# Rows handed one by one into the preparation of the second and fourth graph layers, folded score vectors, and one block for the first layer's preparation

## What is computed

```python
for L in range(4):
    x = x + gnn[L](layernorm(x), adj, ...)
    x = x + ffn[L](layernorm(x), ...)      # top 2 of 16, 8, 8, 16 experts
```

```python
# layer 1, 4 heads of 64
h = x @ W.T; e = leaky_relu((h . a_src)[:, None] + (h . a_dst)[None, :], 0.2)
out = softmax(where(adj > 0, e, -inf)) @ h
# layer 3, twice: with e and with -e
h = x @ W;  e = leaky_relu(h @ a[:256] + (h @ a[256:]).T, 0.2)
out = elu(concat(softmax(e) @ x, -softmax(-e) @ x) @ wtrans)
```

## Time and profile before

| | |
|---|---|
| median of 3 runs | 1176.76 us (1168.61 to 1181.09) |
| the profiled execution, its own time | 1179.99 us |
| its span, first to last instruction | 1178.3 us |
| busy PE, DVE, ACT, POOL over the span | 953.0, 717.9, 491.4, 450.4 us |
| granted TensorE clock, mean | 0.894 of full |

### The profile page before, as it was taken

How to read it: one execution, slowest core, us unless ns; L and a number is a source line. 1 busy time by engine, 2 the same in 40 slices (tenths; PEclk the granted TensorE clock), 3 DMA queues, 4 the chain that set the end, 5 groups by cost and what they waited for, 6 DMA issues and landing times. The chain is left out here.

```text
span 1178.3 us, 23190 instructions
## 1 busy us (share of the span) xinstructions
PE 953.0 (81%) x7338; PEld 885.7 (75%) x7338; DVE 717.9 (61%) x1674; ACT 491.4 (42%) x926; POOL 450.4 (38%) x464
## 2 busy tenths in 40 slices
PE   5785978628788959884998999999658994999993
PEld 1584878625688959873898989999645883899992
DVE  4686555484777655656664546665454786466664
ACT  2151655400555526651204467776414451244341
POOL 1152664310877626640032015553103542344541
PEclk9795998959888669997998999999869996999997
DMA  6005865320000042746224001129420004656853
GB/s 233 1 28 175 294 217 175 115 63 1 6 10 10 6 162 73 254 139 202 62 86 166 11 14 36 45 64 341 166 77 1 10 14 179 250 171 199 283 182 125
DMA packets 63164, 136.85 MB, mean 116 GB/s; under 512 B 10704, under 2 KB 41200, under 8 KB 58352
## 3 DMA queue, kind: packets, MB, share of 16 engines
q1 hardware_dynamic: 54064, 111.24, 27.6%
q0 software_dynamic: 9024, 24.65, 6.9%
HBM read 201.64 MB, written 17.56 MB: 186 GB/s over the span
## 5 line engine op out<-in xcount | busy, mean ns | idle before, releaser
L1694 PE MATMUL r_pH<-e_xsT,e_w 128*128 128x128 f32 x2304 | 283.2, 281 | 25.0 <-DMA e_w<-w_in 16.3
L1694 PEld LDWEIGHTS r_pH<-e_xsT,e_w 128*128 128x128 f32 x2304 | 273.1, 197 | 28.7 <-issue 28.4
L1648 POOL DMA_INDIRECT y_rows<-e_ys,e_to x94 | 150.7, 1603 | 229.2 <-DVE e_idx L1791 109.3
L1803 DVE TENSOR_TENSOR e_w_lo<-e_w,e_w_hi 128x1024 fp32r<-128x1024 f32 (+1 forms) x94 | 137.8, 1466 | 41.5 <-ACT e_w_hi L1751 31.7
L451 PE MATMUL g_o<-g_V,g_pT 128*128 128x65 f32 (+2 forms) x896 | 145.6, 320 | 4.1 <-ACT g_pT L410 4.1
L1709 PE MATMUL r_pY<-e_w_hi,e_h_hi 128*128 128x256 f32 x464 | 140.9, 304 | 7.1 <-issue 6.3
L1658 POOL DMA_INDIRECT e_xs<-xn_rows,e_idx x94 | 105.3, 1120 | 99.5 <-DVE e_idx L1791 73.6
L1751 ACT ACTIVATE e_w_hi<-e_w 128x1024 fp32r<-128x1024 f32 (+1 forms) x94 | 117.1, 1246 | 62.1 <-DMA e_w<-w_in 60.8
L451 PEld LDWEIGHTS g_o<-g_V,g_pT 128*128 128x128 f32 x896 | 132.8, 208 | 11.8 <-ACT g_pT L410 5.1
L1709 PE MATMUL r_pY<-e_w_lo,e_h_hi 128*128 128x256 f32 x464 | 132.7, 286 | 0.0
L1709 PE MATMUL r_pY<-e_w_hi,e_h_lo 128*128 128x256 f32 x464 | 132.4, 285 | 0.0
(11 more groups left out here) (303 smaller groups left out, 1668.1 us busy)
## 6 DMA issues: line engine op xcount, KB each, us to landing
e_w<-w_in SPq DMA_DIRECT2D x56, 1024.0 KB
e_w<-w_in SPq DMA_DIRECT2D x84, 512.0 KB
e_w<-w_in SPq DMA_DIRECT2D x52, 514.0 KB
e_w<-w_in SPq DMA_DIRECT2D x24, 1028.0 KB
e_b<-b_in SPq DMA_DIRECT2D x76, 128.0 KB
e_w<-y_rows SPq DMA_DIRECT2D x32, 256.0 KB, 5.3
p_adj<-adj_in SPq DMA_DIRECT2D x8, 512.0 KB, 7.2
xn_rows<-xn SPq DMA_DIRECT2D x32, 128.0 KB, 1.7
```

The lines of the kernel that those rows point to most:

```text
L1648: pool.indirect_dma_start(out=y_rows[:, :], in_=ys[b][:, :], in_offset=None, out_offset=bass.IndirectOffsetOnAxis(ap=to[b][:, :], axis=0))\
L1694: ins = nc.tensor.matmul(pH[b % 2][:, f, :], w1[b][:, at:at + P], xsT[b % 2][:, c, :], start=(c == 0), stop=(c == DC - 1))
L1803: nc.vector.tensor_tensor(w2_lo[b % 2][:, :], w2[b][:, :], w2_hi[b % 2][:, :].bitcast(F32), ALU.subtract).then_inc(w2_split, 1)
```

## The change

1. Layer 0: constants and preparation are one block. SP issues x, Wn1, neighT, Wv, Wx1, Wfx and the adjacency; ACT issues the 19 small loads on its own queue. PE starts with a run of 64 matmuls on ones, takes neighT's network first, and puts the value matmuls between the transposes. Values and the passed-on half of x are taken from one PSUM tile by instructions over all 8 row tiles.
2. Layer 0's experts to layer 1 (`BeforeGraph1`) and layer 2's experts to layer 3 (`BeforeGraph3`): the weights of the next graph layer are loaded before the wait for the last stores. The weighted sum, the norm, the transposes and the projections then run row tile by row tile at the end of the expert block. The preparation blocks are gone.
3. Layer 1's score vectors are folded into the weights: 4 small matmuls make `wa`, and the dst rows come from xnT by 8 matmuls of 128 columns for each tile (`wab`). hT is no longer computed. ACT empties PSUM in place of DVE. POOL does the power, one column at a time; DVE adds eps.
4. Layer 3: V is projected in the handover, not at the head of the attention block.
5. w1_own, w2_own and b2_own (layer 2) share one tile, in which layer 3's V later lies.

Layers 1 to 2 and the end keep their sum as it was (`PlainSums`, `LastLayer`).

```diff
+class WeightedSum:
...
+def add(self, dve, link, t, acc, base):
+    dve.wait_ge(self.loaded[t], 16)
+    link(nc.vector.scalar_tensor_tensor(out=acc, in0=self.yg[t][:, 0, :], scalar=wts[:, 0, t:t + 1],
+                                        in1=base, op0=ALU.mult, op1=ALU.add))
+    nc.vector.scalar_tensor_tensor(out=acc, in0=self.yg[t][:, 1, :], scalar=wts[:, 1, t:t + 1],
+                                   in1=acc, op0=ALU.mult, op1=ALU.add).then_inc(self.ready, 1)
...
+class Handover:
...
+    def rows(self, dve, link):
+        for t in range(NT + 1):
+            if t < NT:
+                self.sums.add(dve, link, t, x[:, t, :], x[:, t, :])
+                dve.wait_ge(self.sums.ready, t + 1)
+                self.norm.moments(dve, t)
+            if t >= 1:
+                self.norm.norm(dve, t - 1)
+    def gpsimd(self, pool):
+        for t in range(NT):
+            self.norm.invert(pool, t)
...
-with Phase("init") as pi:
-    constants(pi, neighT, neigh_loaded)
...
+sp.dma_start(x[:, :, :], A["x"].rearrange("(t p) d -> p t d", p=P)).then_inc(x_loaded, 16)
+sp.dma_start(wn1[:, :, :], split_rows("L0_gnn_Wn1")).then_inc(neigh_loaded, 16)
+sp.dma_start(neighT[:, :, :], split_rows("neighT")).then_inc(neigh_loaded, 16)
+sp.dma_start(wv[:, :, :], split_rows("L0_gnn_Wv")).then_inc(neigh_loaded, 16)
+sp.dma_start(wx1[:, :, :], split_rows("L0_gnn_Wx1")).then_inc(wx_loaded, 16)
+sp.dma_start(wfx[:, :, :], split_rows("L0_gnn_Wfx")).then_inc(wx_loaded, 16)
...
+sp.wait_ge(wx_loaded, 32)
...
+    pe.wait_ge(roused, 1)
+    rouse(tps[1][:, 0, :], 64)
+    pe.wait_ge(neigh_loaded, 48)
...
+    ins.then_inc(n_risen, 1)
+    pe.wait_ge(made, 4)
+    for t in range(NT):
+        pe.wait_ge(xn_ready, t + 1)
+        if t >= 2:
+            pe.wait_ge(xnT_ready, t - 1)
+        for c in range(DC):
+            ins = nc.tensor.transpose(tps[t % 2][:, c, :], xn[:, t, c * P:(c + 1) * P], ident[:, :])
+        ins.then_inc(tp_ready, 1)
+        for c in range(DC):
+            ins = nc.tensor.matmul(psV[:, t, :], neighT[:, c, t * P:(t + 1) * P], wv[:, c, :],
+                                   start=(c == 0), stop=(c == DC - 1))
+    ins.then_inc(valued, 1)
...
+    ins.then_inc(x_risen, 1)
...
+    pe.wait_ge(n_tanhed, 1)
...
+    ins.then_inc(n_again, 1)
+    nc.tensor.matmul(tps[0][0:2 * HID, 0, 0:2], wer[:, :, :], emb[:, :], start=True, stop=True)\
+        .then_inc(e_summed, 1)
...
+    pe.wait_ge(x_tanhed, 1)
...
+    ins.then_inc(x_again, 1)
+    pe.wait_ge(values_kept, 1)
...
+        for c in range(DC):
+            ins = nc.tensor.matmul(psV[:, t, :], xnT[:, c, t * P:(t + 1) * P], wfx[:, c, :],
+                                   start=(c == 0), stop=(c == DC - 1))
+    ins.then_inc(passed, 1)
+    pe.wait_ge(x_cut, 1)
+    pe.wait_ge(e_tanhed, 1)
...
+    ins.then_inc(own_summed, 1)
...
+for dst, src in small:
+    act.dma_start(dst, src).then_inc(small_loaded, 16)
+act.wait_ge(roused, 2)
+nc.scalar.activation(spent[:, :], power[:, 0, :], ACT.Tanh)
+act.wait_ge(small_loaded, SMALL)
+act.wait_ge(n_risen, 1)
+nc.scalar.activation(tn[:, :].rearrange("p (a b) -> p a b", a=2), psB[0:HID, :, :],
+                     ACT.Tanh, bias=cols[0:HID, 2:3]).then_inc(n_tanhed, 1)
 norm_scalar(act, tps, tp_ready, xnT_ready)
...
+dve.wait_ge(xn_ready, NT)
+nc.vector.tensor_tensor(x[:, :, 0:OUT], x[:, :, 0:OUT], bc(rowsb[:, 1:2, :], [P, NT, OUT]), ALU.add)
+dve.wait_ge(valued, 1)
+nc.vector.tensor_tensor(V[:, :, 0:OUT], psV[:, :, :], bc(rowsb[:, 0:1, :], [P, NT, OUT]), ALU.add)\
+    .then_inc(values_kept, 1)
...
+dve.wait_ge(n_rounded, 1)
+cut(na, N_LO, psB, 3)
+dve.wait_ge(f_summed, 1)
+link(nc.vector.tensor_tensor(f01[:, :, :], tps[1][:, :, :], bc(rowsb[:, 2:3, :], [P, 2, OUT]), ALU.add))
 link(nc.vector.tensor_tensor(f01[:, 1, :], f01[:, 1, :], f01[:, 0, :], ALU.subtract))
+dve.wait_ge(x_rounded, 1)
+cut(xa, X_LO, psA, 1).then_inc(x_cut, 1)
+link(nc.vector.tensor_tensor(x[:, :, OUT:D], x[:, :, OUT:D], bc(f01[:, 0:1, :], [P, NT, OUT]), ALU.add))
+dve.wait_ge(passed, 1)
+nc.vector.tensor_tensor(x[:, :, 0:OUT], psV[:, :, :], x[:, :, 0:OUT], ALU.add)
+dve.wait_ge(own_summed, 1)
+nc.vector.tensor_scalar(rest[:, :], tps[0][:, 0, 0:NT], 1.0 - 0.01, None, ALU.mult)
...
+def prefetch(self, sp):
+    sp.dma_start(self.w[:, :, :], A["L1_gnn_WT"].rearrange("(c p) n -> p c n", p=P)).then_inc(self.weights_loaded, 16)
+    sp.dma_start(self.wr[:, :, :], A["L1_gnn_W"].rearrange("(c p) n -> p c n", p=P)).then_inc(self.weights_loaded, 16)
...
+    for dst, name in ((self.gamma, "L0_ffn_gamma"), (self.beta, "L0_ffn_beta")):
+        sp.dma_start(dst[:, :], A[name].unsqueeze(0).to_broadcast([P, D])).then_inc(self.post_loaded, 16)
...
+def tensor(self, pe):
+    pe.wait_ge(self.weights_loaded, 48)
+    pe.wait_ge(self.parted, 2)
...
+    ins.then_inc(self.folded, 1)
+    pe.wait_ge(self.spread, 1)
+    rouse(self.spare, 56)
+    for t in range(NT + 1):
+        if t < NT:
+            self.norm.turn(pe, t)
+        if t >= 1:
+            self.project(pe, t - 1)
+def project(self, pe, t):
...
+    pe.wait_ge(self.norm.xnT_ready, t + 1)
+    if t >= 2:
+        pe.wait_ge(self.columns_kept, t - 1)
+    for h in range(H):
+        for c in range(DC):
+            ins = nc.tensor.matmul(self.pd[t % 2][:, h, :], self.wab[:, c, h, :], xnT[:, c, q],
+                                   start=(c == 0), stop=(c == DC - 1))
+    ins.then_inc(self.columns, 1)
+    if t >= 2:
+        pe.wait_ge(self.values_kept, t - 1)
+    for c in range(DC):
+        nc.tensor.matmul(self.pv[t % 2][:, 0:D], xnT[:, c, q], self.w[:, c, :], start=(c == 0), stop=(c == DC - 1))
+    for c in range(DC):
+        ins = nc.tensor.matmul(self.pv[t % 2][:, D:D + H], xnT[:, c, q], self.wa[:, c, :],
+                               start=(c == 0), stop=(c == DC - 1))
+    ins.then_inc(self.valued, 1)
...
+def keep(t):
+    act.wait_ge(self.columns, t + 1)
+    nc.scalar.activation(self.dst[:, :, t * P:(t + 1) * P], self.pd[t % 2][:, :, :], ACT.Copy)\
+        .then_inc(self.columns_kept, 1)
+    act.wait_ge(self.valued, t + 1)
+    nc.scalar.activation(self.rest[:, t, :], self.pv[t % 2][:, D:D + H], ACT.Copy, scale=1.0 - SLOPE)
+    nc.scalar.activation(self.V[:, t, :, 0:DH], self.pv[t % 2][:, 0:D].rearrange("p (h d) -> p h d", h=H),
+                         ACT.Copy).then_inc(self.values_kept, 1)
...
+dve.wait_ge(self.folded, 1)
+nc.vector.tensor_copy(self.wa[:, :, :], self.pw[:, :, :, 0])
+nc.vector.tensor_copy(self.wab[:, :, :, :], bc(self.pw[:, :, :, 1:2], [P, DC, H, P])).then_inc(self.spread, 1)
+nc.vector.memset(self.V[:, :, :, DH:DH + 1], 1.0)
...
+link(nc.vector.tensor_tensor(x[:, :, :], x[:, :, :], bc(self.beta[:, :].unsqueeze(1), [P, NT, D]), ALU.add))
+def summed(t):
+    z = self.z[:, t, :]
+    self.sums.add(dve, link, t, z, xn[:, t, 0:D])
+    dve.wait_ge(self.sums.ready, t + 1)
+    link(nc.vector.bn_stats(out=self.p_stats[:, t, :], in_=z))
+    link(nc.vector.bn_aggr(out=self.p_moments[:, t, :], in_=self.p_stats[:, t, :]))
+    nc.vector.tensor_scalar(self.p_moments[:, t, 1:2], self.p_moments[:, t, 1:2], EPS, None, ALU.add)\
+        .then_inc(self.p_var_ready, 1)
+def raised(t):
+    z = self.z[:, t, :]
+    link(nc.vector.scalar_tensor_tensor(out=z, in0=z, scalar=self.p_moments[:, t, 0:1], in1=self.gamma[:, :],
+                                        op0=ALU.subtract, op1=ALU.mult))
+    dve.wait_ge(self.p_rstd_ready, t + 1)
+    nc.vector.scalar_tensor_tensor(out=x[:, t, :], in0=z, scalar=self.p_rstd[:, t:t + 1], in1=x[:, t, :],
+                                   op0=ALU.mult, op1=ALU.add).then_inc(self.x_ready, 1)
+    dve.wait_ge(self.x_ready, t + 1)
+    link(nc.vector.bn_stats(out=stats[:, t, :], in_=x[:, t, :]))
+    link(nc.vector.bn_aggr(out=mean_var[:, t, :], in_=stats[:, t, :]))
+    nc.vector.tensor_scalar(mean_var[:, t, 1:2], mean_var[:, t, 1:2], EPS, None, ALU.add)\
+        .then_inc(self.norm.var_ready, 1)
+for t in range(NT + 2):
+    if t < NT:
+        summed(t)
+    if 1 <= t < NT + 1:
+        raised(t - 1)
+    if t >= 2:
+        self.norm.norm(dve, t - 2)
...
+    pe.wait_ge(self.spread, 3)
+    rouse(self.spare, 56)
+    for t in range(NT + 1):
+        if t < NT:
+            self.norm.turn(pe, t)
+        if t >= 1:
+            pe.wait_ge(self.norm.xnT_ready, t)
+            q = slice((t - 1) * P, t * P)
+            for c in range(DC):
+                ins = nc.tensor.matmul(self.pd[:, t - 1, :], self.wab[:, c, :], xnT[:, c, q],
+                                       start=(c == 0), stop=(c == DC - 1))
+            if t % (NT // 2) == 0:
+                ins.then_inc(self.columns, 1)
+            for c in range(DC):
+                ins = nc.tensor.matmul(self.pq[:, t - 1:t], xnT[:, c, q], self.wa[:, c, 0:1],
+                                       start=(c == 0), stop=(c == DC - 1))
+            if t == 1:
+                pe.wait_ge(self.wt_loaded, 32)
+            if t >= 3:
+                pe.wait_ge(self.placed, t - 2)
```

(29 more changed lines are left out.)

820 lines of the change are left out of this document (339 added, 481 removed).

## The result

| | before | after |
|---|---|---|
| median of 4 | 1177.9 us (1168.6 to 1181.1) | 1143.57 us (1142.7 to 1147.2) |
| ratio | | 0.9727, 95% interval 0.9668 to 0.9786 |
| profiled execution, span | 1178.3 us | 1141.8 us |

The change is worth 2.7% by the ratio of the means (34.3 us between the medians), and 36.5 us between the two profiled spans. The forecast was 1144. That agreement is better than the working behind it, as the table of stages shows. A stage here ends with an event that both kernels have: the first mask of an attention, the first gather of rows for the experts, the last row store. The second pair are two later executions, both on another chip. Its experts' stages of layers 0 and 1 are slower, for both kernels.

A forecast was written before the change was run, and what follows sets the result against it. Stretches between stages were taken as chains of one engine after another; savings of 14.6 + 12.5 + 6.0 = 33.1 us gave 1146.9 profiled, 1144 for the median. Range 1137 to 1150, or 1132 to 1161 with three rivals.

The forecast's parts named there:

- Layer 0, 14.6 us: Layer 0's preparation: first attention matmul at 37.4 us instead of 52.0, saving 14.6 us; 13.0 to 17.0 by the loads' landing.
- I take 6, so the small loads are there at 15.3: Layer 0: last small load issued at 9.3, landing after 6 us (bounds 3.6 and 7.6), which starts the chain with ACT's tanh.
- ACT's tanh after 18: Layer 0: a stated sign that the prediction is wrong, if ACT's tanh started later than 18 us.
- a sum 2.4 us better: Layer 0: if DMA engines take turns between queues, small loads escape SP's 6 MB and land after 3.6 us, 2.4 better.
- Layer 1, 12.5 us: Handover from layer 0's experts to layer 1: first mask at 279.7 instead of 292.16, saving 12.5 us; 10 to 15.2 otherwise.
- PE sets the end: Layer 1's handover: PE's 3.3 us per tile, started at the lower clock (2.75 us), sets the end, at 277.4.
- Layer 3, 6.0 us: Handover from layer 2's experts to layer 3's first `weigh`: saves 6.0 us; 10.5 with clock up, 3 with POOL's waits.
- the 1.8 us for the first `weigh`: Layer 3's attention: PE starts cold, which costs the first `weigh` half of its 3.63 us, 1.8 us.
- Clock kept: Rival: folds and idle matmuls hold PE at the upper clock in the handovers; with early small loads 1134 us, chance 0.14.
- Oscillates in the handovers: Rival: PE rests between tiles and stays at 1.2 GHz in the handovers; 1199 us, slower than before, chance 0.05.
- DVE and POOL set the pace: Rival: linked steps slow the handover tiles and small loads land late, losing 3, 3 and 2 us; 1151 us, chance 0.15.
- Given back: Rival: attention stages start cold and lose the lead; layer 3 gains nothing, the others lose 4 us each; 1158, chance 0.12.

The follow-up runs named there:

- experiment 1: Changed kernel with SP issuing the adjacency only after ACT's small loads have landed: 1144.2 us, ratio 0.9693; layer 0's first mask at 40.2 us instead of 44.4.
- experiment 7: Changed kernel with the 19 small loads on SP's queue, ahead of the adjacency, instead of on ACT's: median 1151.8 us, ratio 0.9724.
- experiment 8: Changed kernel with 190 and 100 idle matmuls before the handovers, next tile's transposes between score columns and V projection: median 1151.7 us, ratio 0.9723.
- run 11: Changed kernel with adjacency behind small loads, 118 idle matmuls starting layer 0, 100 before layer 3's handover with experiment 8's order there: 1146.4 us, ratio 0.9671.
- run 12: Run 11 plus 20 idle matmuls after every fourth unit, from the fifth on, in layer 1's attention: median 1143.1 us, ratio 0.9639.
- run 5: Changed kernel without any idle matmuls in front of the two handovers (0 instead of 56 and 56): median 1155.5 us, ratio 0.9762.

## Why the prediction was right, and where it was not

**The number.** It is right partly by luck. For the profiled execution the working gave 1146.9, and it took 1143.64. The forecast came to 1144 because the 3.2 us by which before's profiled execution stood above its median were taken off, while the changed kernel's stood at its median. And the three places saved 3.1 us less than was forecast, while stages that the working left out saved 6.4.

**Layer 0, 14.6 us: 8.4, two terms mis-sized and one left out.** The failing step is "I take 6, so the small loads are there at 15.3". The broadcast took 9.1 us, outside both bounds (3.6 and 7.6), ACT ended its issuing at 10.58 and not 9.3, and its tanh came at 19.23. Of the 5.8 us between 37.4 and 43.16, that is 3.9, and the passes of x at the lower clock (5.47 against 3.6) are 1.9. The step counted the adjacency only as something that masks might wait for, not as 4 MB that slow the loads issued beside it; experiment 1 prices that at 2.6 us. It would not have been right with loads at 15.3 either: PE's product with neighT, which the sum left out, ended at 17.1. The marker "ACT's tanh after 18" was the one to watch. The prediction cited the Trainium skill, DMA: Bandwidth & Descriptors, section Queues, rings and completion order, for the DMA engines' taking turns between queues packet by packet; from that it made a sum 2.4 us better. It came out worse: 9.1 us on ACT's queue under the adjacency, 3.5 without it, and an earlier finish on SP's own queue in experiment 7. How a DMA engine chose between the queues no run here shows.

**Layer 1, 12.5 us: right in size (13.3), partly wrong in its reason.** PE's tile took 3.27 us (3.3 forecast), the first xn came 14.6 us after the last store (15.3 by the estimate). DVE's round was 3.56 us until the first norm and 3.88 after it (4.0). The step that fell is "PE sets the end", with 2.75 us lost to a cold start. PE has 0.6 us of reserve per tile, had made up the late start by tile 4, and waited for DVE again there and at tile 5 (0.16 and 0.45 us, another of the signs of being wrong). So DVE's round sets the time up to tile 5's xn, and behind it PE's own order: experiment 8 took 1.7 us off there. From the first xn to the first mask the forecast had 35.4 us and the trace has 35.2, so the loss that wasn't paid and the waits that weren't priced came out even. The low clock lasted 10 us, over the 6 that the prediction called a sign of being wrong, and cost nothing.

**Layer 3, 6.0 us: 8.3, inside its range** (8.2 to the first `weigh`, which is what the forecast counted to). PE's tile took 2.83 us (2.84). PE did set the end here: DVE's round was 1.89 us, not 2.3, and of DVE's instructions only the last xn waited for POOL, 0.76 us (844.08), when PE was tiles behind. POOL's steps took 0.29 to 0.36 and 0.57 to 0.78 us, so none had a wait of the size of the earlier trace rows (1.14 us). By the Trainium skill, SBUF — State Buffer, section SBUF: two separate sides, a DVE instruction with two SBUF inputs can hold up a GpSimd instruction that reads SBUF for its whole length. Here that length is 0.48 us; whether a POOL step waited so, these rows don't tell, and PE's pace would have covered it. The term that was too dear is the 1.8 us for the first `weigh`: 3.78 us against 3.63 before. Mask to `weigh` took 10.9 as forecast. The cold start cost 1.7 us (runs 11 and 12; in the changed kernel tile 0's work took 4.62 us against 2.83) and not 2.75, and PE's order, which had no term, about as much again: from the first xn to the first mask experiment 8 took 26.4 us instead of 29.8.

**What no term covered.** 6.4 us of the first pair lie in other stages, 2.8 of them in the last experts' stage (1.6 in the second pair), where the clock fell in one kernel and not in the other. Another 1.7 are in layer 0's experts, a stage that took 110.1 to 116.5 us over these profiles. That they filled what layer 0 lacked is luck. "The expert loops and attention steps aren't touched" was true of the code, not of their time.

**The rivals.** None came true as a whole. *Clock kept*: no, both handovers began at 1.2 GHz; it would have been worth nothing in layer 1 and 1.7 us in layer 3. *Oscillates in the handovers*: the clock came back and stayed. *DVE and POOL set the pace*: DVE does in layer 1, without the loss that was feared, but its small loads that land late came true, at 3.9 us instead of 2. *Given back*: no, each attention kept its lead. The clock does fall and come back in layer 1's attention, in both kernels: it fell behind a rest of 1.23 us, and the same 16 matmuls took 3.26 and 3.51 us instead of 1.90 (timeline of the changed kernel). The Trainium skill, TensorE: Matmul & The Clock Gate, section HAM oscillation, tells of a kernel whose clock falls in each of its waits for DMA, which are longer than this rest. In kind the attention agrees with it; in the handovers the clock came back and stayed.

```profile
308.10 1.90 PE L506 MATMUL g_o<-n_V,g_pT 128*128 128x65 f32 x16
309.84 0.56 PE L235 MATMUL g_front_psl<-g_front_gw,xnT 128*128 128x8 f32 x4
311.63 1.09 PE L495 MATMUL g_tp<-ident,g_lm 128*128 128x128 f32 x8 [1.23 <-DVE g_lm L417]
312.56 3.26 PE L506 MATMUL g_o<-n_V,g_pT 128*128 128x65 f32 x16
315.61 1.91 PE L495 MATMUL g_tp<-ident,g_lm 128*128 128x128 f32 x8
317.32 3.51 PE L506 MATMUL g_o<-n_V,g_pT 128*128 128x65 f32 x16
```

Over the fourteen profiles that stage took 144.7 us at a mean clock of 0.89, 145.8 at 0.83, 147.2 to 148.7 at 0.79 to 0.81, 150.6 and 152.5 at 0.76 and 154.6 at 0.74.

**Still open:** why PE pauses at the head of the last experts' stage in the kernel before, when the clock falls in layer 3's handover and when not, what delays the first y tile by up to 2 us, and what moves layer 2's experts by 3 us in some executions (runs 1, 5, 8 and 12: 178.6 to 180.4 against 175.7 to 177.5).

## What to carry to other kernels

Handing tiles on singly paid only through the overlap here. Follow each engine's round tile by tile to the last one, since the limit can change hands on the way, and look at the consumer's own order: a transpose of tile t+1 ahead of the work of tile t makes the engine wait at the start and leaves more work behind the last tile. When loads are moved to another queue, ask what else is in flight beside them, not only what is in front of them. Where PE rests for about a microsecond again and again, a few idle matmuls in the rests can pay (3.3 us of a stage of 148 here). Put them where the wait is: a run that ended 8 us ahead of the first tile left nothing, and one that ended 1 us ahead of it lost the clock in the next wait. To judge an edit to a stage, measure from an event inside it: from the last store, experiment 8 seemed to gain nothing in layer 1.

## What the runs showed of the hardware

- A 64 KB broadcast on ACT's queue took 9.0 to 9.4 us from issue to landing (seven profiles) while 4 MB of adjacency were under way on SP's, and 3.0 to 3.5 us when they were not (runs 1, 11 and 12).
- The granted clock fell behind rests as short as 1.23 us inside a stage with PE busy 88%, and 20 idle matmuls after every fourth unit raised the mean from 0.85 to 0.97 over the same stretch.
- A start at the lower clock cost nothing in layer 1's handover, where DVE's round (3.88 us) is longer than PE's (3.27) and PE had caught up by tile 4, and 1.7 us in layer 3's, where it is shorter (1.89 against 2.83).
- The granted clock also fell with no rest of PE longer than 0.5 us: behind 4 us in which PE was busy 1.63 (head of the last experts' stage, kernel before, first profile). The first expert block behind it took 5.36 and 5.34 us in the two profiles of that kernel, and 3.81 in both of the changed one.
